# 16-head attention of a four-layer kernel: scores with keys on the partitions, row maxima from a diagonal matmul

## The chip, the cores and the metric

The kernel runs on one core of a Trainium2 chip. The metric is the device time of one execution in microseconds. Before the change it is 800.03 us, the median of three runs (799.91 to 800.35).

## The reference

Four layers change x (4 batches of 256 rows of 128): a gated 4-head mLSTM, an attention with routed projections, the 16-head cross attention that the change is about, and a layer of 8 experts. Cut to the third:

```python
x = x + tanh(g_xattn[1]) * L1_xattn(ctx, mask, layernorm(x))
# L1_xattn: DIM 128, HEADS 16, DIM_HEAD 64
x   = layernorm(features) * gm + bm            # 256 context rows
lat = layernorm(latents) * gl + bl             # 256 rows of x
q, k, v = lat @ Wq, concat(x, lat) @ Wk, concat(x, lat) @ Wv
sim = q @ k.T / 8                              # per head 256 x 512
sim = where(mask, sim - max(sim), -inf)        # the mask covers the 256 context keys
out = softmax(sim) @ v
return out @ Wo
```

All is f32 in the reference. The kernel splits most operands into a high f16 half and a low f16 half and makes each product of three matmuls: high x high, high x low, low x high.

## The kernel before

Everything is written by hand for five engines, which meet only at semaphores. Each engine has its own program, and within a stage these programs are written as functions: `pe_c`, `act_c`, `dve_c` and `pool_c` are TensorE, ScalarE, VectorE and POOL (GpSimd) in the 16-head attention, stage C. Stages A and B (the first two layers) lie before it, stage D (the experts) behind.

Stage C works through 4 batches x 16 heads x 2 query tiles = 128 units. A unit is one head and 128 queries against 512 keys, queries on the partitions. The units run in a software pipeline, one `step` each, in a loop over batches that is split in the middle (`SPLIT_AT`). In step t:

- TensorE makes the scores of unit t+1 (`scores`, lines 951 to 953, three matmuls of 64 rows and 512 columns into one of two banks), the values of unit t-3 (lines 1016 to 1018, twelve matmuls of 65 columns), perhaps one projection (Q, K or V of a head pair or key tile, `project`), and the four transposes of unit t-1 (`turn`, line 1632, f32, 128x128).
- VectorE adds the mask to the scores, scales and negates them and finds the row maximum in one pass (line 1196, `sm`, `nm`), subtracts for the low halves of a projection (line 1174) and of the transposed exponentials (line 1204, `PTl`), and every fourth step divides the values by their sums (`ao`, line 1218).
- ScalarE exponentiates `sm` in f32 into `Pr` (line 1109), copies the high half of the transposed exponentials `PTh` (line 1102), of projections (line 1089) and the transposed outputs `aoT` (line 1094).
- POOL splits the expert weights at the start of the stage (lines 1596 and 1598, eight times a high and a low half) and is then idle.

The order on every engine is the order in the code:

```python
scores(b, t + 1, last)                 # TensorE, step t
# values of unit t - 3, then projections, then:
for j in range(KT):
    ins = turn(bank[:, j * P:(j + 1) * P], m.Pr[:, u % 2, j * P:(j + 1) * P])
```

The output projection (`project_ao`, line 998) is two blocks of eight f32 matmuls per batch. PSUM has eight banks: two for projections, two for scores, two for transposes, two for values.

## Time and profile before

| what | before |
|---|---|
| median of the runs | 800.03 us |
| span of the profiled execution, first to last instruction | 798.0 us |
| profiled execution against the median | its span lies 2.0 us under it |
| mean granted TensorE clock | 0.903 |
| busy PE, VectorE, ScalarE, POOL | 651.7, 635.4, 355.3, 272.4 us |
| stage C, first matmul to the first of the experts | 393.56 to 694.08 us |

Busy is the time in which an engine has an instruction under way. Matmuls are pipelined: one is shown with its whole way through the array (0.38 us for 512 columns), while the next starts 0.2 us later. So for TensorE the starts are read, not the durations. Durations on VectorE and ScalarE overlap with the next instruction by nearly 0.1 us. "PEld" is the weight load of a matmul. "issue" stands where a wait has no releaser in the profile. L951 is line 951 of the program.

### The profile page before, as it was taken

The page shows a single profiled execution, that of the slowest core. Times are in us where ns is not written, and L with a number is a line of the kernel's source. Part 1 is how long each engine was busy: PE and PEld are TensorE (multiplying, and loading weights), DVE is VectorE, ACT ScalarE, POOL GpSimd, SP SyncE. Part 2 cuts the span into 40 slices and gives each one's busy share as a digit, 9 for nine tenths or more (in the row PEclk, how much of TensorE's full clock was granted, in tenths as well). Part 3 has the DMA queues.
Part 4 walks back from the last instruction along what each step waited for, and adds up shares of the span by engine and source line. Part 5 has one row for each costly group of instructions (what it writes and reads, how often), then busy time and mean ns, then how long its engine had stood idle before and what let it go on. Part 6 is the DMA issues. An engine that isn't in the chain of part 4 may idle for free. (4 is left out here: it accounts for less than half of the span.)

```text
span 798.0 us, 16645 instructions
## 1 busy us (share of the span) xinstructions
PE 651.7 (82%) x5465; PEld 405.4 (51%) x5465; DVE 635.4 (80%) x1391; ACT 355.3 (45%) x657; POOL 272.4 (34%) x253
## 2 busy tenths in 40 slices
PE   6499757797488388472589999999999999889997
PEld 5376511443254154252245556655655665557675
DVE  5747899579869969959489887888688879478887
ACT  2432200421231141131257777677677757546652
POOL 4433355146537727664058000000000000046663
PEclk9999968689599689665599999999999999989999
DMA  6211000000000000020013000000000000000000
GB/s 200 67 33 54 28 0 0 1 1 1 0 1 0 0 0 0 0 79 0 1 40 95 1 2 2 1 0 0 0 0 0 0 1 2 1 1 0 0 0 27
DMA packets 13111, 12.75 MB, mean 16 GB/s; under 512 B 2080, under 2 KB 10896, under 8 KB 13072
## 3 DMA queue, kind: packets, MB, share of 16 engines
q1 hardware_dynamic: 13072, 12.25, 5.2%
q8 instruction: 22, 0.36, 0.2%
q14 instruction: 17, 0.14, 0.1%
HBM read 11.72 MB, written 0.52 MB: 15 GB/s over the span
## 5 line engine op out<-in xcount | busy, mean ns | idle before, releaser
L1632 PE MATMUL bank<-ident,work 128*128 128x128 f32 x788 | 127.5, 292 | 8.9 <-DVE work L1832 3.0
L1632 PEld LDWEIGHTS bank<-ident,work 128*128 128x128 f32 x788 | 98.2, 151 | 29.2 <-issue 6.2
L1204 DVE TENSOR_TENSOR PTl<-bank,PTh 128x512 f16<-128x512 f32 x128 | 87.7, 685 | 28.2 <-ACT PTh L1102 27.7
L1567 POOL TENSOR_SCALAR rs<-mv 128x2 f32<-128x2 f32 (+2 forms) x12 | 2.4, 198 | 311.6 <-DVE mv L1775 311.6
L1109 ACT ACTIVATE work<-sm,nm 128x512 f32<-128x512 f32 x128 | 92.0, 719 | 10.9 <-DVE nm L1196 9.7
L1196 DVE CUSTOM_DVE_ANT_0 sm<-bank,maskrow 128x512 f32<-128x512 f32 x128 | 87.2, 681 | 7.1 <-ACT work L1109 5.7
L711 DVE TENSOR_TENSOR work<-bank,gatev 128x512 f32<-128x512 f32 x120 | 79.0, 682 | 14.5 <-PE bank L464 14.1
L1102 ACT ACTIVATE PTh<-bank 128x512 f16<-128x512 f32 x128 | 76.1, 594 | 29.0 <-PE bank L1632 26.7
L462 PE MATMUL bank<-weights,xbTh 128*128 128x512 f16 x120 | 49.4, 412 | 29.1 <-DVE work L711 27.2
L1016 PEld LDWEIGHTS bank<-work,PTh 128*128 128x128 f16 x512 | 46.0, 97 | 52.8 <-issue 47.1
L1328 DVE TENSOR_TENSOR work<-work 128x512 f16<-128x512 f32 x64 | 57.1, 949 | 13.0 <-POOL work L1390 13.0
L1390 POOL TENSOR_SCALAR work<-work 128x512 f16<-128x512 f32 x64 | 53.0, 851 | 36.6 <-ACT work L1322 34.0
L1016 PE MATMUL bank<-work,PTh 128*128 128x65 f16 x512 | 61.2, 196 | 2.1 <-DVE PTl L1204 2.1
L1017 PE MATMUL bank<-work,PTh 128*128 128x65 f16 x512 | 60.2, 195 | 0.0
L487 PE MATMUL bank<-kTh,qTh 64*128 64x256 f16 x64 | 21.3, 347 | 47.5 <-ACT work L628 38.4
L1018 PE MATMUL bank<-work,PTl 128*128 128x65 f16 x512 | 59.6, 193 | 0.0
L628 ACT ACTIVATE work<-bank,nm 128x256 f32<-128x256 f32 x64 | 26.7, 472 | 63.0 <-DVE nm L736 63.0
L951 PE MATMUL bank<-k2h,q2h 64*128 64x512 f16 x128 | 49.5, 387 | 3.3 <-DVE q2l L1174 2.1
L839 POOL TENSOR_TENSOR work<-work 128x512 f32<-128x512 f32 x24 | 30.5, 1270 | 63.2 <-DVE work L711 60.9
L464 PE MATMUL bank<-weights,xbTl 128*128 128x512 f16 x120 | 49.3, 411 | 0.0
L463 PE MATMUL bank<-weights,xbTh 128*128 128x512 f16 x120 | 49.2, 410 | 0.0
L953 PE MATMUL bank<-k2h,q2l 64*128 64x512 f16 x128 | 48.2, 376 | 0.0
(269 smaller groups left out, 1804.7 us busy)
## 6 DMA issues: line engine op xcount, KB each, us to landing
stage<-in_L_ffn_w SPq DMA_DIRECT2D x8, 512.0 KB, 3.8
stage<-in_L_ffn_Wkv SPq DMA_DIRECT2D x4, 640.0 KB, 4.0
stage<-in_L_ffn_Wq SPq DMA_DIRECT2D x2, 640.0 KB, 4.8
xt<-in_x SPq DMA_DIRECT2D x1, 512.0 KB, 4.1
ct<-in_ctx SPq DMA_DIRECT2D x1, 512.0 KB, 5.4
wo<-in_L_xattn_Wo SPq DMA_DIRECT2D x1, 512.0 KB
stage<-in_L_xattn_Wv SPq DMA_DIRECT2D x1, 512.0 KB, 3.4
stage<-in_L_xattn_Wq SPq DMA_DIRECT2D x1, 512.0 KB, 3.4
```

Of the source, the lines that this page charges most:

```text
L711: dve.tensor_tensor(heads8(m.prod[:, k, e, :]), heads8(bank_pj[c % 2][:, :]), wide(g, DH1), ALU.mult).then_inc(s.prod_ready, 1)
L951: pe.matmul(o, ah, bh, start=True, stop=False)
L1016: pe.matmul(o, ph, vh, start=(j == 0), stop=False)
L1017: pe.matmul(o, ph, vl, start=False, stop=False)
L1018: ins = pe.matmul(o, pl, vh, start=False, stop=(j == KT - 1))
L1102: act.activation(m.PTh[:, u % 2, :, :].rearrange("p n c -> p (n c)"), bank_T[use % 2][:, :], ACT.Copy).then_inc(s.c_T_hi, 1)
L1109: act.activation(m.Pr[:, t % 2, :], m.sm[:, t % 2, :], ACT.Exp, scale=-1.0, bias=m.nm[:, t % 4, 0:1]).then_inc(s.c_exp_done, 1)
L1196: dve.tensor_tensor_reduce(m.sm[:, t % 2, :], bank_S[t % 2][:, :], m.maskrow[:, :], -(DH2 ** -0.5), 3e38, ALU.add, ALU.min, m.nm[:, t % 4, ...
L1204: dve.tensor_tensor(m.PTl[:, u % 2, :, :].rearrange("p n c -> p (n c)"), bank_T[use % 2][:, :], m.PTh[:, u % 2, :, :].rearrange("p n c -> ...
L1328: dve.tensor_tensor(m.hTl[:, a, f, :], m.hf[:, use % HR, :], m.hTh[:, a, f, :], ALU.subtract).then_inc(s.h_lo, 1)
L1390: pool.tensor_scalar(m.hTh[:, use // FT, use % FT, :], m.hf[:, use % HR, :], 1.0, 0.0, ALU.mult, ALU.add).then_inc(s.h_hi, 1)
L1632: return pe.transpose(dst, src, m.ident[0:src.shape[0], 0:src.shape[0]])
```

## The change

The scores are computed with the keys on the partitions, so that their exponentials need no transpose before they meet the values. The unit of work is now a head pair (2 heads, 256 queries, 512 keys in four tiles), 32 steps instead of 128.

- **Maxima.** A softmax with keys on the partitions can't reduce along a row for its maximum. So `row_max` makes approximate scores with queries on the partitions, from the high halves alone (one matmul of 512 columns for each head), and adds the mask by a matmul with `first_row`. VectorE takes the maxima of two heads in one reduction over two banks (`take_max`), and writes each as a diagonal 128x128 matrix in bf16 (`spread_max`, four per pair). A matmul of ones with that diagonal subtracts the maximum of each query from all its keys in PSUM (line 1045).
- **Scores.** `scores_T` makes four key tiles in two halves, three matmuls of 64 rows and 256 columns for each head, the two heads in turn: rows 0 to 63 into one bank, rows 64 to 127 into another.
- **Exponentials.** ScalarE reads each tile twice from PSUM (`exps`): once into f32 (`Pf`), once into f16 (`Ph`), with the mask of the key as bias for the two context tiles. The tiles go in three rounds of 512, 512 and 1024 elements. POOL subtracts for the low half `Pl` (`low_exps`), three instructions a step.
- **Gone** are the transposes of exponentials, `sm`, the copies to `PTh`, and VectorE's subtraction for `PTl`. VectorE, not ScalarE, copies the transposed outputs.
- **Banks.** Two for projections, four for scores, two (6 and 7) for the maxima. Bank 6 is also that of the values, bank 7 that of the output projection. TensorE therefore makes the values of pair t-1 only after VectorE has taken both maxima of pair t+1 (`c_max_done`).
- **Projections.** Q is made for two head pairs at a time, every other step; transposed outputs take that place in the odd steps. K comes every step, V in nearly every step.
- **POOL.** Of the eight expert weight splits, four (`N_EARLY`) move to the end of stage B, two of them each behind a `latent_rstd`; four run before the first subtraction.
- A second load of the mask (`mask_col8`, 1024 single bytes) puts keys on partitions; two small constants are added.

```diff
+N_EARLY = 4
-        bk = [stack.enter_context(nc.psum_tensor(f"bank{i}", [P, 512], F32)) for i in range(8)]
+        banks = stack.enter_context(nc.psum_tensor("banks", [P, 8, 512], F32))
+        bk = [banks[:, i, :] for i in range(8)]
...
-                    latent_rstd(0)
-                    latent_rstd(1)
+                    for k in range(2):
+                        latent_rstd(k)
+                        split(N_W1 + 2 + k)
...
-            for n in range(N_W0, N_W1):
+            for n in range(N_W0, N_W1 + 2):
+                if n == N_W1:
+                    pool.wait_ge(s.pj_ready, B * X1)
                 split(n)
...
+        bank_pj2, bank_kq, bank_rm = bk[0:2], bk[2:6], bk[6:8]
+        bank_out, bank_wo = bk[6], bk[7]
...
+            def row_max(it, p, i):
...
+                else:
+                    pe.wait_ge(s.c_max_done, it * PAIRS + (2 * p + 1))
+                for h in range(2):
+                    r = slice(DH2 * h, DH2 * h + DH2)
+                    pe.matmul(bank_rm[h][:, :], m.q2h[r, p % 4, i * P:(i + 1) * P], m.k2h[r, p % 2, :], start=True, stop=False)
+                for h in range(2):
+                    r = slice(DH2 * h, DH2 * h + DH2)
+                    ins = pe.matmul(bank_rm[h][:, 0:S], m.first_row[r, :], m.maskrow[r, :], start=False, stop=True)
+                ins.then_inc(s.c_M_ready, 1)
+
+            def scores_T(it, p, half):
+
+                if p >= 1:
+                    pe.wait_ge(s.c_exp_done, it * EXPS + (3 * (p - 1) + 2 + half))
+                pair = bank_kq[2 * half:2 * half + 2]
+                for k in range(2):
+                    kt = 2 * half + k
+                    for x in range(3):
+                        for h in range(2):
+                            r = slice(DH2 * h, DH2 * h + DH2)
+                            key = (m.k2h, m.k2l, m.k2h)[x][r, p % 2, kt * P:(kt + 1) * P]
+                            q = (m.q2h, m.q2h, m.q2l)[x][r, p % 4, :]
+                            pe.matmul(pair[h][:, k * S:(k + 1) * S], key, q, start=(k == 0 and x == 0), stop=False)
+                if half == 0:
+                    pe.wait_ge(s.c_D_ready, it * PAIRS + (2 * p + 2))
+                for h in range(2):
+                    less = m.diag[:, p % 2, h * S:(h + 1) * S].unsqueeze(1).to_broadcast([P, 2, S])
+                    ins = pe.matmul(pair[h][:, :].rearrange("p (k c) -> p k c", k=2), m.onesb[:, :], less, start=False, stop=True)
+                ins.then_inc(s.c_S_ready, 1)
+
+            def values(it, p, t):
+
+                pe.wait_ge(s.c_P_lo, it * EXPS + (3 * p + 3))
+                if t < STEPS_C - 1:
+                    pe.wait_ge(s.c_max_done, it * PAIRS + (2 * t + 4))
...
+            def step(it, t):
+                jobs, b, n = c_jobs(t), t // HP2, t % HP2
+                scores_T(it, t, 0)
+                if t + 1 < STEPS_C:
+                    row_max(it, t + 1, 0)
+                if "c" in jobs:
+                    job(it, (t, "c"), jobs["c"])
+                scores_T(it, t, 1)
+                if t + 1 < STEPS_C:
+                    row_max(it, t + 1, 1)
+                if "f" in jobs:
+                    job(it, (t, "f"), jobs["f"])
+                if t >= 1:
+                    values(it, t - 1, t)
+                if b >= 1 and n in (2, 4):
+                    project_ao(it, n // 2 - 1, job_no[t - 1, "c"], bank_wo)
+                if "h" in jobs:
+                    job(it, (t, "h"), jobs["h"])
...
+            def exps(it, p, r):
+
+                act.wait_ge(s.c_S_ready, it * PAIRS + (2 * p + r // 2 + 1))
+                if p >= 1:
+                    act.wait_ge(s.c_P_lo, it * EXPS + (3 * (p - 1) + r + 1))
...
+                act.activation(full, src, ACT.Exp, scale=DH2 ** -0.5, bias=bias)
+                act.activation(hi, src, ACT.Exp, scale=DH2 ** -0.5, bias=bias).then_inc(s.c_exp_done, 1)
...
+            def take_max(it, p, i):
+
+                dve.wait_ge(s.c_M_ready, it * PAIRS + (2 * p + i + 1))
+                dve.tensor_reduce(m.nmax[:, p % 2, i, :], banks[:, 6:8, :], AX.X, ALU.max, negate=True).then_inc(s.c_max_done, 1)
+
+            def spread_max(it, p, i):
+
+                dve.wait_ge(s.c_max_done, it * PAIRS + (2 * p + i + 1))
+                for h in range(2):
+                    at = (h * I + i) * P
+                    ins = dve.tensor_scalar(m.diag[:, p % 2, at:at + P], m.identb[:, :], m.nmax[:, p % 2, i, h:h + 1], None, ALU.mult)
+                ins.then_inc(s.c_D_ready, 1)
...
+            def low_exps(it, p):
+                for r in range(3):
+                    kts = slice(r, r + 1) if r < 2 else slice(2, 4)
+                    pool.wait_ge(s.c_exp_done, it * EXPS + (3 * p + r + 1))
+                    pool.tensor_tensor(m.Pl[:, p % 2, kts, :], m.Pf[:, kts, :], m.Ph[:, p % 2, kts, :], ALU.subtract).then_inc(s.c_P_lo, 1)
```

VectorE's step calls `take_max` and `spread_max` for the first query tile of pair t+1, then the low half or copy of the middle job ("c"), then both for the second tile, then divides the values of pair t-1, then the low halves of K and V.

On VectorE in the loop of stage C, two units before (`REGISTER_ALU` rows, which set waits, stand between some; `ISA` is the masking and maximum pass and its read of the accumulator):

```order
L1196 ISA sm,nm<-bank,maskrow 128x512
L1196 ISA nm 128x1
L1174 TENSOR_TENSOR q2l<-bank,q2h 128x256
L1204 TENSOR_TENSOR PTl<-bank,PTh 128x512
L1196 ISA sm,nm<-bank,maskrow 128x512
L1196 ISA nm 128x1
L1204 TENSOR_TENSOR PTl<-bank,PTh 128x512
```

and one whole head pair (four units' worth) now:

```order
L1254 REGISTER_ALU
L1255 TENSOR_REDUCE nmax<-banks 128x2
L1262 TENSOR_SCALAR diag<-identb,nmax 128x128 x2
L1230 REGISTER_ALU
L1234 COPY work<-banks 128x512
L1254 REGISTER_ALU
L1255 TENSOR_REDUCE nmax<-banks 128x2
L1262 TENSOR_SCALAR diag<-identb,nmax 128x128 x2
L1274 REGISTER_ALU
L1277 RECIPROCAL den<-banks 128x4
L77 REGISTER_ALU
L1281 TENSOR_TENSOR work<-banks,den 128x2x64 x2
```

The diagonal blocks of the first tile now stand ahead of the middle job's copy and of the second reduction.

On TensorE, one of the first steps of stage C now (a Q job in the middle; its six matmuls and the K job's three follow the maxima):

```order
L1040 MATMUL banks<-q2l,k2h 128x256 x2
L1045 MATMUL banks<-diag,onesb 128x512 x2
L1022 MATMUL banks<-k2h,q2h 128x512 x2
L1025 MATMUL banks<-maskrow,first_row 128x256 x2
L955 MATMUL banks<-kvTh,wq1h 128x256
L956 MATMUL banks<-kvTl,wq1h 128x256
L957 MATMUL banks<-kvTh,wq1l 128x256
```

Where a transpose of exponentials stood in each unit before (`L1632 MATMUL bank<-ident,work 128x128 x4`), there is none; each half of the scores ends in the two diagonal matmuls, and the maxima of the next pair follow them.

## Rows read from the trace of the kernel before

**Rows 1.** Stretches of core 0: busy us (x instructions) of each engine, PEclk, DMA.
```profile
520.00:560.00 40.00, 40.00 (x414) 23.91 (x414) 34.66 (x88) 30.39 (x55) 0.00 (x0) 1.00 0.00 0
393.56:694.08 300.52, 291.60 (x2920) 176.06 (x2921) 243.90 (x621) 209.25 (x373) 28.79 (x22) 0.99 0.03 10
```

**Rows 2.** Waits, 440 to 640 us: engine, line, released by: us, times, longest.
```profile
PEld bank L1016 <- issue: 35.6, 84, 0.4
ACT PTh L1102 <- PE bank L1632: 20.3, 23, 2.4
DVE PTl L1204 <- ACT PTh L1102: 19.4, 39, 2.3
```

**Rows 3.** TensorE's timeline (start, us): an output projection (weight loads), then one unit.
```profile
503.44 1.86 PEld L998 LDWEIGHTS bank<-wo,work 128*128 128x128 f32 x16 [0.42 <-issue]
...
521.14 0.39 PE L951 MATMUL bank<-k2h,q2h 64*128 64x512 f16 x1
521.37 0.38 PE L952 MATMUL bank<-k2l,q2h 64*128 64x512 f16 x1
521.59 0.38 PE L953 MATMUL bank<-k2h,q2l 64*128 64x512 f16 x1
521.90 0.20 PE L1016 MATMUL bank<-work,PTh 128*128 128x65 f16 x1
...
522.27 0.63 PE L1632 MATMUL bank<-ident,work 128*128 128x128 f32 x4
522.84 0.39 PE L951 MATMUL bank<-k2h,q2h 64*128 64x512 f16 x1
```

**Rows 4.** Groups of lines, 440 to 640 us: form, count, busy us, mean ns, idle.
```profile
L1109 ACT ACTIVATE work<-sm,nm 128x512 f32<-128x512 f32 x90 | 64.7, 719 | 0.3
L1204 DVE TENSOR_TENSOR PTl<-bank,PTh 128x512 f16<-128x512 f32 x90 | 61.7, 686 | 19.9 <-ACT PTh L1102 19.4
...
L1174 DVE TENSOR_TENSOR k2l<-bank,k2h 128x512 f16<-128x512 f32 x23 | 15.9, 691 | 6.3 <-ACT k2h L1089 6.3
...
L1089 ACT ACTIVATE k2h<-bank 128x512 f16<-128x512 f32 x22 | 13.1, 597 | 11.9 <-PE bank L953 11.9
...
L1174 DVE TENSOR_TENSOR q2l<-bank,q2h 128x256 f16<-128x256 f32 x23 | 9.6, 419 | 0.0
...
L1089 ACT ACTIVATE q2h<-bank 128x256 f16<-128x256 f32 x23 | 8.8, 383 | 6.5 <-PE bank L953 6.5
```

**Rows 5.** Groups of lines of the whole span, VectorE and ScalarE.
```profile
L736 DVE TENSOR_REDUCE nm<-bank 128x2 f32<-128x512 f32 x32 | 21.7, 682 | 4.0 <-PE bank L489 3.5 <-issue 0.4
...
L628 ACT ACTIVATE work<-bank,nm 128x256 f32<-128x256 f32 x64 | 26.7, 472 | 63.0 <-DVE nm L736 63.0
```

**Rows 6.** Lines of POOL's subtractions: ns min/median/max, first and last start us.
```profile
L1606 POOL TENSOR_TENSOR kvTl<-sm,kvTh x2: 1152/1576/2000, 23.2 to 25.9; 128x512 f16<-128x512 f32 x2
...
L1598 POOL TENSOR_TENSOR wv1l<-stage,wv1h x1: 2122/2122/2122, 344.3 to 344.3; 128x1024 f16<-128x1024 f32 x1
```

**Rows 7.** One line of VectorE, then the timeline of POOL and VectorE there.
```profile
L1889 DVE TENSOR_SCALAR n<-xt,mv,rs x8: 334/339/2541, 58.8 to 111.7; 128x128 f32<-128x128 f32 x8
...
58.69 2.60 POOL L1598 TENSOR_TENSOR weights<-stage,weights 128x1280 f16<-128x1280 f32 x1
...
58.84 2.80 DVE L1889 TENSOR_SCALAR n<-xt,mv,rs 128x128 f32<-128x128 f32 x2 [0.81 <-POOL rs L1568]
```

**Rows 8.** Timeline, 324 to 337 us: VectorE alone, then beside POOL.
```profile
324.91 3.78 DVE L769 TENSOR_TENSOR work<-work,topm 128x512 f32<-128x512 f32 x5
...
328.77 2.88 POOL L861 TENSOR_TENSOR work<-work 128x1280 f32<-128x1280 f32 x1 [3.04 <-DVE work L769]
...
329.21 7.42 DVE L769 TENSOR_TENSOR work<-work,topm 128x512 f32<-128x512 f32 x5
```

**Rows 9.** Timeline of TensorE at the start of the stage.
```profile
394.37 0.64 PE L953 MATMUL bank<-wv1h,kvTl 128*128 128x512 f16 x1
394.80 0.64 PE L951 MATMUL bank<-wv1h,kvTh 128*128 128x512 f16 x1
```

More of the change, by code:

```diff
@@ L926, in jobs @@
-        def jobs(t, last):
-            job = projection(t, last)
-            if job and last and job[2]:
-                slot = t // 4 - KT
-                return [(job[0], "norm", 0, slot, 0)] if job[1] == "v" and slot < len(NORM_TILES) else []
-            return [job] if job else []
-        PAST_JOB = (PJ0 - 1, "v", 0, KT - 1, 0)
-        FIRST_JOBS = [(n, "v", 0, n, 0) for n in range(KT - 1)] + [(KT - 1, "qk", 0, 0, 0), (KT, "qk", 0, 0, 1), (KT + 1, "v", 0, KT - 1, 0)]
+        STEPS_C = B * HP2
@@ new lines, in build, with three @@
+        PJ, PJ_HI = 3 * HP2, 3 * HP2 - 2 * I
+        for t in range(SPLIT_AT, STEPS_C - HP2 - 3):
+            assert all(job_no[t + HP2, p] == job_no[t, p] + PJ and hi_no[t + HP2, p] == hi_no[t, p] + PJ_HI for p in "cfh")
+        N_JOBS = len(job_no)
+        PAIRS, EXPS = 2 * HP2, 3 * HP2
+        def three(pe, o, ah, al, bh, bl):
+            pe.matmul(o, ah, bh, start=True, stop=False)
+            pe.matmul(o, ah, bl, start=False, stop=False)
+            return pe.matmul(o, al, bh, start=False, stop=True)
@@ L1050, in pe_c @@
-            for t in range(SPLIT_AT, UN + 3):
-                step(B - 1, t, last=True)
-            for p in range(TILES_AO):
-                turn_ao(B, p, p - TILES_AO)
+            def step(it, t):
[16 more added lines that the diff above has]
+                    job(it, (t, "h"), jobs["h"])
@@ new lines, in pe_c @@
+            for p, j in enumerate(BEFORE):
+                job(0, (-1, p), j)
+                if p == 1:
+                    row_max(0, 0, 0)
+                if p == 2:
+                    row_max(0, 0, 1)
+            for t in range(SPLIT_AT):
+                step(0, t)
+            with pe.Fori(0, B - 1) as it:
+                for t in range(SPLIT_AT, SPLIT_AT + HP2):
+                    step(it, t)
+            for t in range(STEPS_C - HP2 + SPLIT_AT, STEPS_C):
+                step(0, t)
@@ L1113, in act_c @@
-            for job in FIRST_JOBS:
-                high(0, job)
-            for t in range(SPLIT_AT):
-                step(0, t, first=True)
-                if t == LAT_AT + 2:
-                    latent_high(act, B - 1)
-            with act.Fori(0, B - 1) as b:
-                for t in range(SPLIT_AT, UN):
-                    step(b, t)
-                for t in range(SPLIT_AT):
-                    step(b + 1, t)
-            for t in range(SPLIT_AT, UN + 2):
-                step(B - 1, t, last=True)
@@ L1381, in pool_d @@
         def pool_d(pool):
[L1382 removed]
+            pool.wait_ge(s.c_O_ready, STEPS_C)
             with pool.Fori(0, E3) as e:
```

560 lines of the change are left out of this document (294 added, 266 removed).

## Prediction

> **What bounds the kernel now.** I read the stretches first. In the steady part of the 16-head attention TensorE is busy for all of 40 us, at granted clock 1.00, while VectorE has 34.7 us of work and ScalarE 30.4; the stage as a whole lasts 300.5 us [rows 1]. A busy PE proves little, since the ends of matmuls are modelled, so the waits come next: VectorE waits 19.4 us for ScalarE's high halves and ScalarE 20.3 us for transposes, and TensorE's largest wait has no releaser, only "issue" [rows 2]. The timeline of a unit (one head, 128 queries) without other jobs shows what that is: three score matmuls start 0.22 us apart, twelve value matmuls take 0.37 us from first to next, four transposes 0.43 us, and about 0.1 us passes each time the form goes from 64\*128 to 128\*128 or back (521.59 + 0.21 = 521.80 against 521.90) [rows 3]. Together that is the 1.70 us to the next unit. So TensorE bounds this stage, by start-to-start pitch: 0.215 us for 512 columns, 0.108 for 256, 0.107 for a transpose, 0.031 for a value matmul, 0.11 for a change of form. A head pair (4 units) takes about 8.9 us on average, with projections, two changes of form per unit and, per pair, a quarter of a block of the output projection, 1.77 us each (1.86 for its 16 weight loads, less the last one's overlap) [rows 3].
>
> **What the change does to TensorE, per head pair.** Gone: 16 transposes, 16 x 0.107 = 1.71 us. Scores: 24 matmuls of 256 columns are as many columns as 12 of 512, 2.59 us if one runs after the other. Now they alternate between rows 0 to 63 and 64 to 127 of the array and between two banks. No stretch of this trace has such neighbours. The bounds: 2.59 us one after the other, 1.30 us if neighbours run side by side. I take 1.30: the form 64\*128 of the score matmuls [rows 3] is half the array at the full pitch of 512 columns, so the other half stands free, and the pause at each change of form says that the array is truly split. The same holds for the row maxima (4 matmuls of 512 and 4 of 256 columns): 1.29 us or 0.65, taken 0.65. The diagonal matmul needs all 128 rows: 4 x 0.215 = 0.86. Changes of form stay at 8 (0.9 us). Values stay at 48 x 0.031 = 1.46, K and V projections at 0.65 each, Q at half of 0.65, turned outputs at half of 0.43. TensorE's sum is then 1.30 + 0.65 + 0.86 + 0.9 + 1.46 + 1.29 + 0.54 = 7.0 us, and 7.3 with the output projection, 1.5 us per pair under today's.
>
> The Trainium skill (TensorEngine Tiling (Array Packing), Theoretical Speedup) gives up to 2x for a contract dimension of at most 64, which is the lower bound above; no run here shows it yet.
>
> **The other engines, per head pair.** ScalarE drops 4 exponentials of 719 ns and 4 copies of 0.60 us [rows 4] and gets 4 exponentials of 512 elements and 2 of 1024. From PSUM 256 elements take 472 ns [rows 5], and 256 more add 0.21 us (383 against 597 for the copies to q2h and k2h) [rows 4]: 0.69 and 1.11 us, less 0.1 of overlap with the next. With the copies of projections that is 4.4 + 1.25 = 5.6 us, hidden. VectorE drops 8 passes of 0.68 us and gets two maxima over 1024 elements (682 ns for 512 [rows 5], plus 0.54 for as many again, from twice 691 - 419 ns [rows 4]: 1.22, pitch 1.14) and four diagonal blocks: 5.6 us, hidden in sum. POOL, idle in this stage today, subtracts 2 x 512 and 1 x 1024 elements: 1.15 and 2.12 us [rows 6], 1.2 and 2.2 with the gaps, 4.6 us. So every sum is under 7.3, and the order decides.
>
> **The wait that comes in.** The PSUM bank of the row maxima is also that of the values. TensorE can start values(t-1) only when VectorE has taken the second maximum of pair t+1; behind this wait stand the values, the V projection and the next scores. One step, from its start: scores 0.65, form, diagonal 0.43 (1.19), form, first maxima 0.32 (1.62); landing after a matmul 0.21 (a copy starts that long after the stream ends). VectorE reduces from 1.84 to 3.10 (1.14 and 0.13 of handover). Meanwhile ScalarE does the first two exponentials from 1.40 to 2.56, and POOL's first subtraction runs from 2.71 to 3.91. At 3.10 VectorE wants to write the diagonal: a tensor_scalar from SBUF to SBUF with a per-partition scalar. Such an instruction took 2541 ns against 334, started 0.15 us behind a POOL subtraction of 2.60 us and ended with it [rows 7]. So I let it wait until 3.91; two blocks (0.19 each, a third of the 0.34 and 0.27 that two-scalar f32 ones need taken off) end at 4.29, the copy of turned outputs at 4.89, the second reduction hands over at 6.16. TensorE had been ready at 4.67. Then values 1.46, V projection 0.65, form 0.11: **8.38 us a step**. Even steps (Q instead of turned outputs) come out alike.
>
> The Trainium skill (SBUF — State Buffer, section SBUF: two separate sides) calls the port pair of VectorE and GpSimd an exclusive lock: the later one blocks for the other's whole instruction. The trace agrees for this operation [rows 7] and not quite for another, since five two-input SBUF passes that started behind a POOL addition of 2.88 us took 7.42 us together instead of 3.78 [rows 8], 1.48 each, less than one such addition. By the rule the step is 8.38 us; by a port that lets VectorE through, 7.60.
>
> **The sum.** Before the first step the six jobs and two maxima take 8.8 us, and since the clock is still at its lower level there (starts 0.43 us apart) [rows 9] 1.3 more. Steps 0 and 1, without values, take 13.7; 29 steps of 8.38 are 243.0; the output projection falls into 6 of them, 6 x 1.77 = 10.6; latents and the last norm disturb two steps, 1.6; the last step with values, two turned blocks, their copies and two output projections takes 15.6. Sum 294.6 us against 300.5: 5.9 gained. Against it, four weight splits move from this stage into the end of the one before, to fill POOL's idle time; two lie beside VectorE's SBUF work there, which is on the path. Such a pass grew from 0.76 us to 1.48 beside POOL [rows 8]. Bounds 0 and 3 us, taken 1.5. The latents' statistics wait for POOL behind subtractions: 0.4, hidden later if at all. The 1024 one-byte packets of the new mask load are queued where nothing waits for tens of us, and the memsets of `onesb` and `first_row` replace one of `maskb`: nothing, covered by POOL's idle time. Net 4.0 us. The profiled execution had a span of 798.0 us, 2.0 under the median of 800.0, which I take as fixed: 794.0 in the span, **796 us**.
>
> **Rivals.** (a) *The port is not held* for the small bf16 block: it slips between POOL's accesses, as [rows 8] half suggest. A step is 7.60 us, 7.82 with a Q job: 29 x 0.67 = 19.4 less, and half of the 1.5 in the earlier stage: **776 us**. Against it: [rows 7] are the same operation. (b) *The halves don't run side by side.* Scores and maxima cost 1.96 us more of TensorE; the port wait then hides in it, and a step takes 9.57: 31 x 1.19 = 37 us more and 2 at the ends, **835 us**. For it: no neighbours in different halves exist in this trace to prove the contrary. It decides once two alternating 256-column matmuls take over 0.13 us together (4.0 / 29 / 6 above 0.108). (c) *POOL's subtraction is slow in company.* Its 512-element row ranges from 1152 to 2000 ns [rows 6]; at the mean of 1576 the diagonal waits to 4.29, each step is 0.38 longer and the ends too: 14 us more, **810 us**, slower. It decides from 1.34 us per subtraction on, where the 4 us are gone. (d) *The reduction or ScalarE is dearer*: 0.1 us per exponential or 0.15 per reduction is 6 us: 802, taken as the forecast's own upper side.
>
> **Chances.** Forecast 0.52 (own range 788 to 804), (a) 0.26, (b) 0.12, (c) 0.10. Faster by over 0.2% (1.6 us, about what a measurement of this kernel can tell from no change) is (a) and two thirds of the forecast: 0.60; within it 0.10; slower is (b), (c) and the forecast's tail: 0.30. The range is 774 to 812: from (a) to (c), leaving out (b) and a little on each side.
>
> **What would show it.** Score matmuls of one pair should start a few ns apart, or 0.108 if (b). The diagonal's tensor_scalar should show durations far over 0.3 us while POOL subtracts; if all are short, (a). TensorE's wait before the values should be released by the maximum, about 1.5 us a step; POOL's 512-element rows should read 1.15. I am wrong in kind if ScalarE or POOL turns out to be waited for by TensorE directly, or if the stage before this one moves by over 3 us.

## The result and the profile after

The change makes the kernel slower: 822.04 us, median of four runs (818.58 to 824.06), against 799.97 us of the kernel before on the same chip. The ratio is 1.0268, with a 95% interval of 1.0241 to 1.0294. I had forecast 796 us and a range up to 812. The profiled execution took 821.55 us, its span is 819.8.

Where the 21.8 us between the two spans lie, by the first matmuls of stage C and of the experts (398.37 and 715.21 now, 393.56 and 694.08 before): stage C 316.8 instead of 300.5 us, 4.8 us in the end of the stage before it, 0.7 in the experts.

The stretches of the kernel after, with the columns of [rows 1]: the stage, a stretch of its steady part, and one single step.

```profile
398.37:715.21 316.84, 260.73 (x3177) 146.82 (x3177) 247.75 (x429) 182.36 (x280) 147.67 (x104) 0.94 0.01 2
460.00:500.00 40.00, 33.03 (x452) 17.89 (x453) 36.10 (x60) 25.13 (x40) 20.18 (x14) 1.00 0.01 2
508.67:519.33 10.66, 8.63 (x96) 4.58 (x94) 8.51 (x13) 5.42 (x8) 4.43 (x3) 0.84 0.01 2
```

TensorE is no longer busy throughout (33.0 of 40 us), VectorE rises to 36.1, and the clock of the stage falls from 0.99 to 0.94. The waits of 440 to 640 us, as in [rows 2]:

```profile
ACT work L1149 <- PE banks L957: 53.2, 21, 4.5
PEld banks L1063 <- DVE nmax L1255: 35.9, 20, 2.6
```

Where TensorE waited for nothing in particular, it now waits for VectorE's second maximum ahead of the values (L1063). The groups of the same stretch, as in [rows 4]:

```profile
L1262 DVE TENSOR_SCALAR diag<-identb,nmax 128x128 bf16<-128x128 bf16 x88 | 56.5, 682 | 1.5
L1255 DVE TENSOR_REDUCE nmax<-banks 128x2 f32<-128x1024 f32 x44 | 53.5, 1216 | 11.2 <-PE banks L1025 10.9
...
L1378 POOL TENSOR_TENSOR attn<-work,attn 128x512 f16<-128x512 f32 x44 | 50.9, 1158 | 91.4 <-ACT attn L1165 91.4
L1378 POOL TENSOR_TENSOR attn<-work,attn 128x1024 f16<-128x1024 f32 x22 | 46.9, 2134 | 16.6 <-ACT attn L1165 16.6
L1164 ACT ACTIVATE work<-banks,maskbias 128x512 f32<-128x512 f32 x43 | 29.6, 688 | 19.5 <-PE banks L1045 19.5
```

The estimated durations are right: the reduction 1216 ns for 1220, POOL 1158 and 2134 for 1150 and 2120, ScalarE 688 for 690. The small diagonal block is what stands out. It has 128 columns and takes 682 ns on average, more VectorE time than the reductions over 1024.

A step is measured here from the first diagonal matmul (L1045) of one head pair to that of the next. The even steps take 8.18 to 8.20 us where nothing else falls into them, close to the forecast 8.38. The odd ones, which I had taken for alike, mostly take 9.18 to 9.20. VectorE in an odd step (first diagonal matmul at 531.29), then POOL in the same step:

```profile
532.37 1.22 DVE L1255 TENSOR_REDUCE nmax<-banks 128x2 f32<-128x1024 f32 x1 [2.39 <-PE banks L1025]
533.63 2.09 DVE L1262 TENSOR_SCALAR diag<-identb,nmax 128x128 bf16<-128x128 bf16 x2
535.64 0.68 DVE L1234 COPY work<-banks 128x512 f32<-128x512 f32 x1
536.24 1.21 DVE L1255 TENSOR_REDUCE nmax<-banks 128x2 f32<-128x1024 f32 x1
...
533.36 2.31 POOL L1378 TENSOR_TENSOR attn<-work,attn 128x512 f16<-128x512 f32 x2 [6.40 <-ACT attn L1165]
```

POOL's two subtractions follow each other without a gap (2.31 us for both), and the two blocks end with the second one (535.72 against 535.67), not with the first. In the even step behind it ScalarE has a Q copy between the exponentials, so POOL has a gap of 0.49 us, and the blocks end in it:

```profile
542.83 1.09 DVE L1262 TENSOR_SCALAR diag<-identb,nmax 128x128 bf16<-128x128 bf16 x2
543.84 0.68 DVE L1249 TENSOR_TENSOR q2l<-banks,q2h 128x512 f16<-128x512 f32 x1
...
542.55 1.16 POOL L1378 TENSOR_TENSOR attn<-work,attn 128x512 f16<-128x512 f32 x1 [4.08 <-ACT attn L1165]
544.20 1.15 POOL L1378 TENSOR_TENSOR attn<-work,attn 128x512 f16<-128x512 f32 x1 [0.49 <-ACT attn L1165]
```

Three more losses show. Where the loop over batches goes back, TensorE stands still for 1.91 us (and 1.49 the next time). No engine holds it: the scores behind it need only exponentials that had ended before 525 us, and VectorE, the last engine at work, is done at 529.98:

```profile
530.53 0.28 PE L1040 MATMUL banks<-q2h,k2h 64*128 64x256 f16 x2 [1.91 <-issue]
```

In four odd steps of the steady part the granted clock falls to the lower level behind TensorE's wait for the maximum. Step 11, from the wait on:

```profile
512.70:514.80 2.10, 0.08 (x1) 0.00 (x1) 2.06 (x4) 1.43 (x3) 1.34 (x2) 1.00 0.00 0
514.80:515.90 1.10, 1.10 (x31) 1.10 (x32) 1.10 (x2) 0.00 (x0) 1.04 (x1) 0.83 0.00 0
515.90:518.90 3.00, 3.00 (x32) 1.69 (x31) 1.42 (x5) 0.54 (x1) 0.00 (x0) 0.50 0.02 5
518.90:526.00 7.10, 6.24 (x90) 3.41 (x86) 5.08 (x8) 5.31 (x9) 3.48 (x3) 1.00 0.02 3
```

At 0.50, which is 1.2 GHz, the end of the values, the V projection and half of the next scores go at half pace: the step takes 10.66 us instead of 9.19. The same happens in steps 1 and 2 and behind the last step. The end of the stage, from the last step's first diagonal matmul to the experts, in the kernel after and then in e2_splits_later, where the clock stays up:

```profile
698.13:715.21 17.08, 13.61 (x163) 11.92 (x163) 6.75 (x21) 5.77 (x10) 4.44 (x3) 0.80 0.01 2
699.56:714.33 14.77, 10.94 (x162) 9.38 (x163) 6.65 (x21) 5.78 (x10) 4.43 (x3) 1.00 0.01 2
```

And at the end of the stage before, VectorE's normalisation of the latents meets the weight splits that were moved there:

```profile
360.14 1.04 POOL L1693 TENSOR_SCALAR weights<-stage 128x1024 f16<-128x1024 f32 x1
361.26 2.13 POOL L1695 TENSOR_TENSOR weights<-stage,weights 128x1024 f16<-128x1024 f32 x1
...
361.03 3.47 DVE L693 TENSOR_SCALAR ct<-xt,mv,rs 128x128 f32<-128x128 f32 x6
...
368.51 4.06 DVE L693 TENSOR_SCALAR ct<-ct,mv,rs 128x128 f32<-128x128 f32 x6 [0.16 <-POOL rs L1665]
```

In the kernel before, without POOL beside them, the same passes (there line 685) are these:

```profile
361.88 1.62 DVE L685 TENSOR_SCALAR ct<-xt,mv,rs 128x128 f32<-128x128 f32 x6
...
367.51 1.62 DVE L685 TENSOR_SCALAR ct<-ct,mv,rs 128x128 f32<-128x128 f32 x6 [0.16 <-POOL rs L1568]
```

### The profile page after: what moved, and what is told of

It is laid out like the page before. It is cut to its first block, busy times and chain, and to the rows that moved or that the text cites. A ratio compares the mean times of both kernels' runs of the same rounds, so it can differ in the third digit from the quotient of the medians.

```text
span 819.8 us, 16271 instructions
## 1 busy us (share of the span) xinstructions
PE 623.1 (76%) x5721; PEld 377.6 (46%) x5721; DVE 644.3 (79%) x1199; ACT 328.5 (40%) x565; POOL 414.4 (51%) x353
## 4 chain that ended last, share of the span: by engine, by line
PE 43%; DVE 39%; issue 10%; ACT 3%; POOL 2%; DVEq 1%; DMA 1%; ACTq 0%; SPq 0%; POOLq 0%; PEld 0%
DVE nmax L1255 8%; DVE work L722 5%; DVE work L780 5%; DVE diag L1262 3%; PE banks L1733 3%; PE banks L1040 2%; PE banks L1063 2%; PE banks L470 2%; PE banks L1071 2%; PE banks L1439 2%; PE banks L1065 2%; PE banks L1064 2%; PE banks L1440 2%; PE banks L1441 2%; PE banks L1045 2%
## 5 line engine op out<-in xcount | busy, mean ns | idle before, releaser
L1378 POOL TENSOR_TENSOR attn<-work,attn 128x512 f16<-128x512 f32 (+1 forms) x96 | 142.1, 1482 | 147.4 <-ACT attn L1165 147.4
L722 DVE TENSOR_TENSOR work<-banks,gatev 128x512 f32<-128x512 f32 x120 | 79.0, 682 | 14.2 <-PE banks L472 13.8
L1255 DVE TENSOR_REDUCE nmax<-banks 128x2 f32<-128x1024 f32 x64 | 77.7, 1215 | 15.3 <-PE banks L1025 14.8
L1063 PE MATMUL banks<-work,attn 128*128 128x65 f16 x512 | 54.4, 200 | 44.9 <-DVE nmax L1255 37.9
L1262 DVE TENSOR_SCALAR diag<-identb,nmax 128x128 bf16<-128x128 bf16 x128 | 81.5, 677 | 2.2
L1063 PEld LDWEIGHTS banks<-work,attn 128*128 128x128 f16 x512 | 48.8, 101 | 59.6 <-DVE nmax L1255 42.5
L470 PE MATMUL banks<-weights,xbTh 128*128 128x512 f16 x120 | 49.6, 414 | 28.0 <-DVE work L722 26.1
L1733 PE MATMUL banks<-ident,work 128*128 128x128 f32 x276 | 53.0, 330 | 8.6 <-DVE work L1933 3.0
L1164 ACT ACTIVATE work<-banks,maskbias 128x512 f32<-128x512 f32 x64 | 44.0, 688 | 35.7 <-PE banks L1045 35.7
L1065 PE MATMUL banks<-work,attn 128*128 128x65 f16 x512 | 54.4, 200 | 0.0
L1064 PE MATMUL banks<-work,attn 128*128 128x65 f16 x512 | 54.3, 200 | 0.0
L1065 PEld LDWEIGHTS banks<-work,attn 128*128 128x128 f16 x512 | 49.4, 102 | 0.0
L1064 PEld LDWEIGHTS banks<-work,attn 128*128 128x128 f16 x512 | 49.3, 101 | 0.0
L472 PE MATMUL banks<-weights,xbTl 128*128 128x512 f16 x120 | 49.3, 411 | 0.0
L471 PE MATMUL banks<-weights,xbTh 128*128 128x512 f16 x120 | 49.2, 410 | 0.0
```

Source lines behind the costliest of these rows:

```text
L470: pe.matmul(o, xh, wh, start=True, stop=False)
L472: pe.matmul(o, xl, wh, start=False, stop=True).then_inc(s.pj_ready, 1)
L722: dve.tensor_tensor(heads8(m.prod[:, k, e, :]), heads8(bank_pj[c % 2][:, :]), wide(g, DH1), ALU.mult).then_inc(s.prod_ready, 1)
L1063: pe.matmul(o, ph, vh, start=(kt == 0), stop=False)
L1064: pe.matmul(o, ph, vl, start=False, stop=False)
L1065: ins = pe.matmul(o, pl, vh, start=False, stop=(kt == KT - 1))
```

## The experiments

The kernel before took between 799.4 and 812.1 us on the chips of the experiments (mean granted clock 0.903 to 0.909 where it took under 802 us, 0.886 to 0.888 where it took over 811). Its median was 805.18 us beside e1 to e4, 800.83 beside e5 to e8, 811.83 beside e9 and e10 and 804.97 beside e11, while my expectations are in times of the first chip (800 before, 822 after). So a few us in the median decide nothing. Ratios are to it, on the same chip; what an edit does is read from the length of stage C in each profile, first matmul to the first of the experts: 300.5 us before, 316.8 after. The steps are typical ones at the higher clock, without an output projection or a way back of the loop. The table gives all, the sections what they mean; the diffs there are shortened.

| run | median us | ratio, 95% interval | stage C us | steps, odd / even us |
|---|---|---|---|---|
| after | 822.04 | 1.0268, 1.0241 to 1.0294 | 316.8 | 9.19 / 8.19 |
| e1_tt_diag | 838.30 | 1.0411, 1.0333 to 1.0490 | 328.8 | 9.30 / 8.33 |
| e2_splits_later | 822.83 | 1.0244, 1.0186 to 1.0303 | 314.9 | 9.18 or 8.20 / 8.19 |
| e3_maxima_first | 795.26 | 0.9898, 0.9845 to 0.9952 | 286.7 | 7.65 / 7.83 |
| e4_heads_apart | 823.47 | 1.0241, 1.0181 to 1.0302 | 311.1 | 8.20 or 9.18 / 8.20 |
| e5_narrow_pool | 789.19 | 0.9869, 0.9794 to 0.9945 | 281.1 | 7.65 / 7.83 |
| e6_heads_far | 831.86 | 1.0393, 1.0323 to 1.0463 | 321.3 | 9.41 / 8.43 |
| e7_maxima_v_first | 786.09 | 0.9774, 0.9709 to 0.9839 | 279.6 | 7.22 / 7.19 |
| e8_all | 782.88 | 0.9758, 0.9695 to 0.9822 | 279.6 | 7.21 / 7.19 |
| e9_tensor_unrolled | 821.06 | 1.0164, 1.0027 to 1.0302 | 313.9 | 9.25 / 8.27 |
| e10_all_unrolled | 777.42 | 0.9606, 0.9509 to 0.9702 | 270.5 | 7.25 / 7.27 |
| e11_one_write | 806.24 | 1.0028, 0.9985 to 1.0072 | 296.7 | 8.26 / 8.27 |

My theory after the result: POOL's subtraction holds off VectorE's diagonal blocks, each block by itself. The rivals: another cause makes the blocks slow, or the wait of TensorE only changes its releaser.

**e1_tt_diag**

```diff
-ins = dve.tensor_scalar(diag, m.identb, m.nmax[..., h:h + 1], None, ALU.mult)
+ins = dve.tensor_tensor(diag, m.identb, m.nmax[..., h:h + 1].to_broadcast([P, P]), ALU.mult)
```

> Theory (the port): in the changed kernel the diagonal's four VectorE blocks of a step wait for POOL's subtractions, each block by itself, so that one of a pair can sit behind two subtractions (2.0 to 2.1 us instead of 0.42 in the odd steps, 1.0 in the even ones). Written as a product of two tensors, with the maximum spread by a stride of 0, the same 128x128 bf16 blocks do not take the lock: all last 0.25 us or less, the second reduction starts when its matmuls have landed (3.5 to 3.7 us after the first diagonal matmul, not 4.95), values start at 4.7 to 4.9 us in every step, steps of 7.7 and 7.9 us instead of 9.19 and 8.19: 822 - 29 x 0.88 - 3 for the first steps = 793 us, 787 to 803. Rival 1 (every VectorE instruction on SBUF is held by POOL, whatever its kind): the new blocks last as long as the old, 820 to 824. Rival 2 (the wait only changes its releaser: ScalarE or the copies of projections come last instead): the blocks are short but the steps keep over 8.4 us, 808 to 818.

Rival 1 came true. The blocks of an even step, with POOL's subtraction beside them:

```profile
551.87 1.23 DVE L1262 TENSOR_TENSOR diag<-identb,nmax 128x128 bf16<-128x128 bf16 x2
...
551.59 1.15 POOL L1378 TENSOR_TENSOR attn<-work,attn 128x512 f16<-128x512 f32 x1 [3.68 <-ACT attn L1165]
```

Both inputs lie in SBUF, and that is enough to be held. So the kind of instruction is no way out. The time is even longer than with the old blocks: free of POOL a pair takes 0.49 us instead of 0.42, steps are 0.1 us longer, no odd step slips through, and in seven odd steps instead of four the lower clock follows (six of 10.8 us and step 29). The copies and low halves that read PSUM (L1234, L1249) last 0.68 us beside POOL as without it. The Trainium skill (SBUF — State Buffer, section SBUF: two separate sides) names both cases for the exclusive lock, a pass in a mode of two ports and one with two inputs from SBUF; by that rule the product is held too, and the trace agrees (1.23 us). I had read only the first half of it.

**e3_maxima_first**

```diff
 take_max(it, t + 1, 0)
-spread_max(it, t + 1, 0)
 low(it, (t, "c"), jobs["c"])
 take_max(it, t + 1, 1)
+spread_max(it, t + 1, 0)
 spread_max(it, t + 1, 1)
```

> VectorE takes both maxima before it writes any diagonal block; nothing else changes. Theory (the port is what delays the second maximum): the second reduction starts when its matmuls have landed, 3.5 to 3.7 us after the first diagonal matmul, and values start at 4.7 to 4.9 us as in the run with the other instruction. But the four blocks now meet POOL's subtraction of 1024 elements (5.05 to 7.2 us) and end at 7.2 to 7.7, when the next scores want them, and the division and the low halves of K come later: half of the gain or all of it is lost again, 800 to 820 us, blocks of up to 2.2 us. Rival (the order alone was at fault, the blocks slip through later): 793 us with short blocks.

The second reduction starts at 3.39 and 3.57 us, values at 4.68 and 4.85, as expected, and stage C is 30.1 us shorter. The meeting with the large subtraction, for which I had allowed up to all of the gain, costs nothing in the steady steps: the blocks start first, and in the odd steps it is POOL that then takes 2.20 us. So 795.26 us lies under my 800 to 820 and near the rival's 793 with short blocks; whether the order alone was at fault, as the rival says, is for e5 to tell, where the order stays.

```profile
541.36 1.23 DVE L1255 TENSOR_REDUCE nmax<-banks 128x2 f32<-128x1024 f32 x1 [0.50 <-PE banks L1025]
542.50 0.73 DVE L1262 TENSOR_SCALAR diag<-identb,nmax 128x128 bf16<-128x128 bf16 x4
...
543.02 2.20 POOL L1378 TENSOR_TENSOR attn<-work,attn 128x1024 f16<-128x1024 f32 x1 [0.68 <-ACT attn L1165]
```

The granted clock was 1.00 from 420 to 660 us here.

**e5_narrow_pool**

```diff
-pool.tensor_tensor(m.Pl[..., kts, :], m.Pf[:, kts, :], m.Ph[..., kts, :], ALU.subtract)
+pool.tensor_tensor(m.Pl[..., kts, 0:16], m.Pf[:, kts, 0:16], m.Ph[..., kts, 0:16], ALU.subtract)
-ins = pe.matmul(o, pl, vh, ...)
+ins = pe.matmul(o, ph, vh, ...)
```

> The changed kernel in its own order, but POOL subtracts only 16 of 256 columns per key tile (the value matmuls read the high half in place of the low one, so the low halves are left out of the result, at the same count and size of matmuls). Theory (POOL's long subtraction is what holds VectorE's small blocks, whatever their instruction): with rows of POOL near 0.1 to 0.2 us all blocks take 0.25 us or less (0.42 for two), the second reduction starts when its matmuls have landed (3.4 to 3.7 us after the first diagonal matmul), steps are 7.65 to 7.9 us as when both maxima are taken first, about 795 us, 785 to 803. Rival (the blocks are slow by their place between two reductions, or the copy of the middle job is): blocks of 1.0 and 2.0 us remain, 815 to 822 us.

Here nothing but POOL's time is taken away, and the order of VectorE stays that of the change. All blocks are short, and the steps are those of e3. ScalarE and TensorE have shorter waits for POOL here too, but e3 leaves those as they are and has the same steps. The two together show the cause.

```profile
535.88 0.42 DVE L1262 TENSOR_SCALAR diag<-identb,nmax 128x128 bf16<-128x128 bf16 x2
536.22 0.68 DVE L1234 COPY work<-banks 128x512 f32<-128x512 f32 x1
536.94 1.23 DVE L1255 TENSOR_REDUCE nmax<-banks 128x2 f32<-128x1024 f32 x1
...
535.61 0.22 POOL L1378 TENSOR_TENSOR attn<-work,attn 128x16 f16<-128x16 f32 x1 [4.10 <-ACT attn L1165]
```

**e11_one_write**

```diff
-for h in range(2):
-    ins = dve.tensor_scalar(diag[h], m.identb, nmax[h], None, ALU.mult)
+ins = dve.tensor_tensor(both, m.identb.unsqueeze(1).to_broadcast([P, 2, P]), wide(nmax, P), ALU.mult)
```

> The changed kernel in its own order, but the two diagonal blocks of a query tile are one VectorE instruction (a product of two tensors, 128x256) instead of two. Theory (each instruction asks for the shared port by itself, and in the odd steps the second block of the first tile comes behind POOL's second subtraction, which follows the first by 0.0 us): with one instruction there is one wait, until 3.15 to 3.25 us after the first diagonal matmul, also in the odd steps. With 0.35 to 0.4 us for its own work it ends at 3.6, the copy of the turned outputs at 4.2, the second reduction starts there instead of at 4.95, and odd steps take 8.3 to 8.5 us instead of 9.19; even steps 8.2 to 8.3 as before. 16 x 0.8 = 13 us less than 822 us: 809, and where TensorE's shorter waits spare it the lower clock, down to 803; range 802 to 813. Rival (POOL's two subtractions are one after the other so tightly that VectorE never comes between, even for one instruction): blocks of 2.0 to 2.3 us in the odd steps remain, 818 to 824 us.

This is what the theory expected, and the run settles the odd steps: those from step 5 to 27 take 8.17 to 8.28 us. POOL still has its two subtractions back to back, but the one instruction comes between them:

```profile
542.94 1.16 DVE L1261 TENSOR_TENSOR diag<-identb,nmax 128x256 bf16<-128x256 bf16 x1
544.02 0.68 DVE L1234 COPY work<-banks 128x512 f32<-128x512 f32 x1
...
542.66 2.45 POOL L1377 TENSOR_TENSOR attn<-work,attn 128x512 f16<-128x512 f32 x2 [2.37 <-ACT attn L1165]
```

POOL's pair grows from 2.31 to 2.45 us: now its second one waits. Stage C takes 296.7 us, 20.1 less: 5.6 in the six steps of 9.2 us, 9.7 in the four in which the lower clock had followed (it is 1.00 from 460 to 700 us now), 3.3 in step 1, and 2.3 behind the last step's first diagonal matmul, where the clock stays up too.

**e2_splits_later**

```diff
-N_EARLY = 4
+N_EARLY = 2
 for k in range(2):
     latent_rstd(k)
-    split(N_W1 + 2 + k)
```

> The two weight splits that stand beside the latents' statistics at the end of the second layer move behind that layer. Theory: they cost two blocked rows of per-partition-scalar passes there (3.21 instead of 1.62 us and 3.81 instead of 1.36, together 4.0 us), on the path; without them the 16-head stage starts 4 us earlier. POOL then has six splits of 3.3 us before its first subtraction instead of four, from 387 to 407 us less the 4, which ends close to that subtraction (411.8 less 4): up to 2 us come back. 818 us, 816.5 to 820. Rival (the rows are slow for another reason, or the path goes elsewhere): 821 to 823.

From POOL's first weight split (346.1 to 346.6 us in e1, e2 and e3) to stage C it is 53.3 us, against 56.8 in e1 and 56.9 in e3, which have the splits; it was 50.4 before and 56.1 in the kernel after. So the two splits cost 3.5 of some 6 us there. The time as a whole can't tell it: 822.83 us is the rival's number and not my 818, and 1.0244 lies within the interval of the change's own ratio. The run shows something else. Without any edit in the steady part of stage C, steps 5, 7 and 13, which take 9.2 us in the kernel after, take 8.2 to 8.3 here, for the second block slips in ahead of POOL's second subtraction. Steps 9, 17 and 27, where it had slipped in there (8.1 us), take 9.1 to 10.7 here. What differs is tiny: in step 5 POOL's second subtraction starts 3.227 us after the first diagonal matmul instead of 3.222, and the second block at 3.192 instead of 3.191. Over the odd steps of after, e2, e4, e6 and e9 the second subtraction starts 0.023 to 0.034 us behind the second block where the block is held, and 0.033 to 0.037 us behind it where it slips in. So thousandths of a us go with 1 us of a step, and what decides within them is open.

**e4_heads_apart and e6_heads_far**

```diff
-for k in range(2):
-    for x in range(3):
-        for h in range(2):
+for k in range(2):
+    for h in range(2):
+        for x in range(3):
```

In e6_heads_far the loop over h is outermost.

> The score matmuls of the two heads are no longer in turn: three of rows 0 to 63, then three of rows 64 to 127. Theory (neighbours in different halves of the array run side by side, as the pairs that start 0.11 us apart say): a half of the scores takes 1.0 to 1.3 us instead of 0.65, and a step becomes longer by 0.65 to 1.2 us, 835 to 860 us in all. Rival (the matmuls do not overlap, the two starts of a pair are only a way of recording): a half of the scores takes what it took, and the time stays at 820 to 824 us.

> All six score matmuls of one head, then all six of the other, in each half of the scores. With three and three the time did not move, and both heads' matmuls still started in pairs. Theory (each half of the array has a queue of its own some matmuls deep, so that the order of the program matters only over a longer reach): with six and six the overlap shrinks, a half of the scores takes 0.9 to 1.3 us instead of 0.65, steps up to 1.2 us longer where TensorE is late, 825 to 855 us. Rival (the order does not matter at this reach either): 820 to 824 us and pairs of starts as before.

In e4 the score matmuls start in pairs 0.11 us apart as before, though the program has three of one head and then three of the other; a half of the scores still takes 0.65 us. My 835 to 860 us did not come, the rival's 820 to 824 did, though its reason (no overlap at all) is ruled out by e6. Stage C is 5.7 us shorter than in the kernel after, and this isn't the edit's: the second block slips in ahead of POOL in eight of the thirteen odd steps from 5 to 29 instead of three, by differences as small as those in e2. With six and six the start pattern changes; one half of the scores in e6:

```profile
554.30 0.28 PE L1040 MATMUL banks<-q2h,k2h 64*128 64x256 f16 x1
554.42 0.27 PE L1040 MATMUL banks<-q2h,k2l 64*128 64x256 f16 x1
554.53 0.27 PE L1040 MATMUL banks<-q2l,k2h 64*128 64x256 f16 x1
554.53 0.37 PE L1040 MATMUL banks<-q2h,k2h 64*128 64x256 f16 x2
...
555.09 0.27 PE L1040 MATMUL banks<-q2l,k2h 64*128 64x256 f16 x1
```

The first three and the last three go alone, so the half lasts 0.88 us (nine starts), and every step is 0.23 us longer. The overlap of the two halves of the array is real, and the second head's matmuls start up to three ahead of their place, not six. My expected 825 to 855 held with its lower end; the 0.88 us for a half lies just under its 0.9.

**e7_maxima_v_first, e8_all**

```diff
+if "h" in jobs: job(it, (t, "h"), jobs["h"])
 values(it, t - 1, t)
 project_ao(...)
-if "h" in jobs: job(it, (t, "h"), jobs["h"])
```

(but for the last step; e3's order on VectorE, with the low halves ahead of the division; e8 also has e2's splits)

> Both maxima first on VectorE, and the V projection goes ahead of the values on TensorE, into its wait for the second maximum; VectorE takes the low halves of K and V ahead of the division. In the run with both maxima first TensorE still waited 0.75 us ahead of the values (ready at 4.1 us, values at 4.68 to 4.86). Theory: the wait takes up the 0.65 us of the projection and steps become 7.05 to 7.25 us instead of 7.65 to 7.85, 29 x 0.6 = 17 us less than there: 778 us, 773 to 786. Rival (the division, now behind two low halves, comes too late for the bank of the maxima, or the low half of K does): steps stay at 7.6 or more, 790 to 800 us with a new wait of the first matmul of the maxima.

> The same with two weight splits moved behind the second layer. If the splits cost what their run says (the 16-head stage started 53.3 us after POOL's first weight split instead of 56.1 to 56.9), this is 2 to 4 us under e7; if what they save comes back at the start of the stage, within 1 us of it.

The steps became 7.0 to 7.2 us as expected, but the time of e7 did not follow to 778 and lies at the upper bound of 786: steps 2 to 4 take 9.3, 10.6 and 8.6 us (the latents' norm stands between), and behind each way back of the loop there is a step of 8.3 to 8.5 us. The last two steps see the lower clock as well (0.76 and 0.75 on average). e8 is 3.2 us under e7. That is less than the intervals are wide, but the profiles show where it comes from: 51.1 us from POOL's first weight split to stage C instead of 56.1, and stage C the same. Part of the 5.0 us is a higher granted clock there, so 3.5 from e2 is the safer size of the two splits. Both runs are under both kernels.

**e9_tensor_unrolled and e10_all_unrolled**

```diff
-with pe.Fori(0, B - 1) as it:
+for it in range(B - 1):
     for t in range(SPLIT_AT, SPLIT_AT + HP2):
         step(it, t)
```

> The changed kernel with the loop over batches in stage C written out on TensorE alone; the other engines keep theirs. In the changed kernel TensorE stood still for 1.91 and 1.49 us, with no releaser, just where the loop goes back (ahead of the scores of steps 13 and 21), while every other engine had finished. Theory (the way back to the start of the loop is what takes this time, in the open because TensorE comes there after waits, with nothing queued): both gaps fall to the 0.1 us of a change of form, steps 12 and 20 go from 11.96 and 11.55 us to about 10.0, 3 to 4 us less in all: 818 us. Rival (another engine's way back, or the fetch of instructions itself, which a longer program does not spare): the gaps stay or move, 821 to 824 us.

> Both maxima first, V ahead of the values, two splits later, and TensorE's loop written out. There the gaps were 2.2 to 2.4 us and a slower step followed each (8.3 to 8.5 instead of 7.2, at a lower granted clock). By the same theory 2 x 3.5 = 7 us less than the 783 us of the run without it: 776 us, 772 to 780; by the rival 781 to 785.

Both gaps go: steps 12 and 20 take 10.06 and 10.05 us, where 11.96 and 11.55 stood. The time alone would speak for the rival (821.06 us, not my 818), and stage C is only 2.9 us shorter: the lower clock comes in steps 13 and 21 now (10.8 us), no more in 11, in 29 and behind the last step, and each step is 0.07 us longer, which I can't explain. So the loop's cost is read from the two steps. In e10, where TensorE hardly waits, all of the gain stays: stage C takes 270.5 us against 279.6 in e8, and 777.42 us lies in my 772 to 780. It is the fastest of all, 3.9% under the kernel before (0.9606, 0.9509 to 0.9702), and each of its six runs (770.53 to 783.65) is under each of the kernel before on that chip (799.85 to 812.14).

The traces also say what the way back waits for, a part of what I had written down as the rival. They hold the fetches of instructions (queue q8, blocks of 16 KB). At each way back of the ten runs with the loop, two of them follow each other closely (525.98 and 527.32 us in the kernel after), and TensorE starts again 1.5 to 1.7 us behind the end of the second, while the gap itself varies from 1.4 to 2.5 us. In e9 and e10 there is one fetch where these two were, and no gap. The kernel before fetches nothing on this queue between 499 and 651 us, while its loop goes back. No run changes the fetches alone, so this is read from their times, not shown by an edit.

## Why the prediction was wrong

By its own steps, predicted and measured in the profile after:

| term | predicted us | measured us |
|---|---|---|
| before the first step | 10.1 | 10.7 |
| steps 0 and 1 | 13.7 | 16.8 |
| the next 29 steps, with 6 output projections, latents and norm | 255.2 | 270.6 |
| last step and end | 15.6 | 18.7 |
| end of the stage before | 1.5 more | 4.8 more |
| experts | 0 | 0.7 more |

- **Right.** The durations of reduction, exponentials and subtractions; the two halves of the array side by side (so not rival b); POOL at 1.16 us in company (not c); the block that is held (not a); the wait ahead of the values, released by the maximum. The even step came out at 8.19 for 8.38 us, and this was partly luck: I had worked the step out with the odd step's copy and without POOL's second subtraction. In the even steps the Q copy on ScalarE happens to keep that subtraction away from the second block; I hadn't reckoned with it.
- **The step that failed** is "So I let it wait until 3.91; two blocks (0.19 each ...) end at 4.29", together with "Even steps (Q instead of turned outputs) come out alike". I counted one wait for two instructions. Each is held for itself, and in the odd steps ScalarE has no Q copy between the exponentials, so that POOL's second subtraction takes the port ahead of the second block. That happened in ten of the odd steps (rows of 2.0 to 2.1 us, or 1.62 where the first block came late): six of 9.2 us, 0.81 over the forecast each, and the four below. Three odd steps (9, 17, 27) slipped through with 8.1 us; step 3, with the latents' transposes in its middle, has short first blocks and takes 9.18 us for another reason. e3, e5 and e11 show the cause. I had every number for it; what I left out was to place POOL's second subtraction beside the second block in an odd step.
- **What hangs on it.** In four of the ten (11, 19, 25, 29) the lower clock followed: 10.0 to 10.7 us, 8.3 us over the forecast together. I had no term for the clock in the steady part. In e11, e3 and e5, whose waits are shorter, it stays at 1.00 there. It does not follow from the wait alone: step 5 has one of 2.11 us and no drop. What decides it is open. Its price is large. An estimate from the rows: 1.6 and 1.2 us in steps 1 and 2 (from the first value matmul to the next step 4.5 and 4.2 us instead of 3.0), 5.8 in the four odd steps (against 9.17, 9.14 and 8.50 us for steps 11, 9 and 29 at the higher clock in e9), 2.3 at the end against e2. Together that is some 11 of the 22 us that stage C lies over my sum.
- **Missing terms.** The way back of the loop, 3.2 us over the forecast in two steps (e9 and e10). Step 2 with 3.0 and steps 0 and 1 with 3.1 us: the latents' statistics on POOL stand ahead of its subtractions, and VectorE's two blocks then take 2.3 us; I had written "0.4, hidden later if at all". Nearly half of these 6.1 us is the lower clock that followed. The end, 3.1 us, has the same start: three subtractions in a row behind the last norm's statistics, and 3.2 us for a pair of blocks. But e2 has the same rows and loses only 0.8 us there (16.4 for my 15.6); the other 2.3 are the lower clock.
- **Mis-sized.** The moved splits, +1.5 with bounds of 0 and 3, measured 4.8. I took the 1.48 us of [rows 8] for a pass that shares the port. One by one the five passes last 2.99, 2.02, 1.36, 0.68 and 0.68 us: the first three were each held until one of POOL's additions had ended (at 331.65, 333.60 and 334.88 us), the others were free. The stretch that I called VectorE alone wasn't quite: its first pass lasts 1.37 us beside POOL's addition from 324.47 to 325.73. So [rows 8] bore out the exclusive port and gave rival (a) no support. The two rows of line 693 are 1.85 + 2.44 = 4.3 us over those of before, most of it in one pass each that POOL held (2.19 and 2.14 us for 0.34); e2 puts the price of the two splits on the path at 3.5 us.
- **The sign.** With 9.19 us for the 14 odd steps among the 29, 11 us more, the forecast would have been 807, slower. So the sign hung on one assumption, that one wait serves both blocks, in a step that I took for both kinds.

e11 gives the check: where only the second wait is taken away, stage C takes 296.7 us, against the 294.6 of the sum; by its terms 10.7, 14.0, 256.4 and 15.5 us, for 10.1, 13.7, 255.2 and 15.6. The 256.4 still hold the loop's gaps and a slow step 2, against steady steps a little under the 8.38, so some of this closeness is luck.

## What to carry to other kernels

When a short VectorE instruction on SBUF stands on the path and POOL works on SBUF, draw both engines' rows for every kind of step, and let each instruction wait for itself; two small ones behind each other can lose to two long ones. The way out is an order in which they start ahead of the long one, or a single instruction, not another kind of instruction. A kernel in which TensorE begins to wait can pay more than the wait: here the lower clock came on top, with some 11 us, and the way back of a loop with 3.2.

## What the runs showed of the hardware

- A product of two SBUF tensors is held by POOL's subtraction like a tensor_scalar (in e1 1.23 us for a pair of blocks in even steps, 2.1 to 2.2 in odd ones, 0.49 free); passes that read PSUM are not (0.68 us in both cases).
- Two small blocks can be held by two subtractions one after the other (2.09 us for the pair); one instruction of both was held by one (1.16 us). Where POOL's second subtraction starts some 0.03 us behind VectorE's second block, thousandths of a us go with 1 us of a step: the same step took 9.2 us in one run and 8.2 in another.
- It costs POOL too: its subtraction of 1024 elements takes 2.20 us instead of 2.12 behind four blocks, and a pair of 512 takes 2.45 instead of 2.31.
- Score matmuls of the two halves of the array overlap also when the program has three of one and then three of the other, and only in part with six and six: 0.65, 0.65 and 0.88 us.
- The way back of a loop left TensorE standing for 1.4 to 2.5 us, and it started again 1.5 to 1.7 us behind the second of two instruction fetches. Nothing shows in the kernel before: between 420 and 650 us TensorE has no gap of 0.9 us or more there, and from 499 us on no fetch of that queue.
- The experts took 103.9 to 104.6 us in the profiles of before, after, e3 and e5, and 107.6 to 107.9 in those of the other runs, with the same code. The mean granted clock of this stage was 0.949 to 0.959 in the first four and 0.932 to 0.949 in e2, e8, e9 and e11, so it can be a part of it; the rest is open.
